# A fused attention and expert kernel on eight cores: who makes -alpha k, and a new order on TensorE, VectorE and ScalarE

## The chip, the cores and the metric

The kernel runs on the 8 cores of one Trainium2 chip. Each core computes two of the sixteen sequences and shares nothing with the others. A core has five engines with queues of their own: TensorE (PE), VectorE (DVE), ScalarE (ACT), GpSimd (POOL) and SyncE (SP), which only issues DMAs here. The metric is the device time in microseconds of the slowest core.

## What is computed

```python
x = x + attention(layernorm(x))
x = x + experts(layernorm(x))

# attention, 16 heads of 64, chunks of 64 tokens
q, k, v = x @ Wq.T, x @ Wk.T, x @ Wv.T;  k = k / max(|k|, 1e-12)
alpha = sigmoid(alpha_raw) * 0.5;  beta = sigmoid(beta_raw) * 2.0
for each chunk:
    attn_out = softmax(causal(q @ k.T / 8)) @ v
    out = attn_out + 0.1 * (q @ M)
    for each token t of the chunk:
        M = M - alpha * outer(M @ k_t, k_t) + beta * outer(v_t, k_t)
out = out @ Wo.T
```

The recurrence over the 64 tokens of a chunk is solved at once: with the strictly lower triangle A of -alpha k k^T, the sum of its powers is applied as (I+A)(I+A^2)(I+A^4)(I+A^8)(I+A^16)(I+A^32).

## The kernel before

The kernel has two phases. Phase A, the attention, takes about 1000 us; phase B, the experts, the rest, and it isn't touched. Phase A runs 32 tiles (NT) of 128 rows, which are one chunk of 64 tokens of both sequences. It is written as a software pipeline in which every engine has its own loop, `for i in range(-1, NT + 3)` (GpSimd's and SyncE's from 0), and an instruction order set out by hand. All order between engines is by counting semaphores. In iteration i an engine works on up to four tiles: it projects tile i (k, v and q, from L495), makes the gram and score products of tile j = i-1, solves tile u = i-2 (powers of A, and their factors) and ends tile e = i-3 (factors 4 and 5, the state, the output product with Wo).

TensorE's order in a full iteration (L714 to L800): k's first half, power_a(1), factor(e,4); k's second half, power_b(1), factor(e,5); v's first half, power_a(2), state_h; half of v's second half, power_b(2), state_m; the rest of v, x_turn (the transpose of the next tile), power_a(3), k_by_h; q's first half, power_b(3), factor(u,0), row_sums; half of q's second half, k_turn, gram_and_scores(j), factor(u,1); the rest of q, wo_part, power_a(4), factor(u,2), q_turn, wo_part, power_b(4), queries, wo_part, power_a(5), factor(u,3), values.

- state_h (from L634, H) makes the update of H from Wf, the result of the last factor, and RHS. VectorE adds it to H_sb (L868). state_m (L647, M) needs the new H_sb's semaphore, since it reuses the PSUM tile psY; VectorE adds it to M_sb (L880). k_by_h (L658) needs both and reads ka_fm, which is -alpha k; VectorE makes RHS of it (L886).
- power_a and power_b (L597) write psX; ScalarE copies them to A[k] and B[k] (L411, L415). VectorE's plus_eye (L825) makes AI[k] = A[k] + I, both inputs in SBUF. factor(u,k) (L630) multiplies with AI[k]; VectorE copies psW to W or, for k = 5, Wf (L829).
- gram_and_scores (L575) writes k k^T and k q^T of every head into the whole of psXY: the heads in row order hrow 0 to 7 into psX, 8 to 15 into psY. Its waits are for -alpha k (s_ka), q_fm, for B[3]'s copy, which frees psX, and for s_lden, the logarithm of the softmax's row sums, which frees psY.
- ScalarE takes the row sums' logarithm and its negative exponential into rden (L475, L477), copies the gram to g_sb (L483), and takes the exponential of the scores into PT (L484), for which power_a(4) waits. ln_steps (L403) are two activations for the layernorm of tile i+2; the norm of k is rk (L459, L461), from VectorE's kss (L871) and its maximum, kmax (L873). o_copy (L435) opens its iteration.
- VectorE's xnf copy (L883) takes x_turn's result and frees psD0 for q's first half. stats and normal (L808 to L811, L817) are the layernorm of tile i+2. k_fm (L898) is the copy of k_turn's result.
- GpSimd multiplies elementwise: PT by the mask (L363), -alpha k (kaq, L367), k squared (L372), k by its norm (kt, L376), Ms_sb = M_sb by beta (L381), Pn = PT by rden (L391), and two masks for A[0] and B[0] (L395, L398). Between them it issues eight DMAs of each tile (cast, L354) that turn the experts' weights into bf16.

## Time and profile before

| | us |
|---|---|
| median of 3 runs | 1400.66 (1400.26 to 1402.19) |
| the profiled execution: time | 1394.15 |
| its span on the slowest core | 1392.3 (cores 1382.8 to 1392.3) |
| TensorE busy over the span | 1148.8 (83%) |
| VectorE, ScalarE, GpSimd busy | 980.6 (70%), 810.8 (58%), 672.1 (48%) |

| stage, us | TensorE busy | VectorE | ScalarE | GpSimd | granted clock |
|---|---|---|---|---|---|
| 360 to 460 | 91.36 | 74.20 | 57.05 | 71.84 | 1.00 |
| 560 to 660 | 89.95 | 71.95 | 56.10 | 71.29 | 1.00 |
| 760 to 860 | 89.44 | 70.97 | 56.42 | 71.51 | 1.00 |
| 1100 to 1392 | 240.21 | 217.07 | 205.98 | 10.30 | 0.93 |

The columns of the second table are the busy time of each engine within the stage. TensorE's granted clock is given as a share of full speed, 2.4 GHz. The attention loop lies between about 64 and 1005 us. An iteration begins with k's first half; the full ones took 27.1 to 31.5 us from one to the next, mostly 27.7 to 29.7. An engine that is not the bottleneck may sit idle at no cost, so the shares of busy time alone don't tell what a change is worth.

### The profile page before, as it was taken

The page shows a single profiled execution, that of the slowest core. Times are in us where ns is not written, and L with a number is a line of the kernel's source. Part 1 is how long each engine was busy: PE and PEld are TensorE (multiplying, and loading weights), DVE is VectorE, ACT ScalarE, POOL GpSimd, SP SyncE. Part 2 cuts the span into 40 slices and gives each one's busy share as a digit, 9 for nine tenths or more (in the row PEclk, how much of TensorE's full clock was granted, in tenths as well). Part 3 has the DMA queues.
Part 4 walks back from the last instruction along what each step waited for, and adds up shares of the span by engine and source line. Part 5 has one row for each costly group of instructions (what it writes and reads, how often), then busy time and mean ns, then how long its engine had stood idle before and what let it go on. Part 6 is the DMA issues. An engine that isn't in the chain of part 4 may idle for free. (4 is left out here: it accounts for less than half of the span.)

```text
span 1392.3 us, 68142 instructions; the slowest of 8 cores (1382.8 to 1392.3 us)
## 1 busy us (share of the span) xinstructions
PE 1148.8 (83%) x28864; PEld 692.5 (50%) x28864; DVE 980.6 (70%) x1389; ACT 810.8 (58%) x1187; POOL 672.1 (48%) x566
## 2 busy tenths in 40 slices
PE   1578988889899988889899888885677779887798
PEld 0245555555555555555555555553344556544665
DVE  3167777677777777777777777765778587785776
ACT  0155656555565555555565555654249776488775
POOL 4166766776767766777667766675101000011000
PEclk9799999999999999999999999996569799988999
DMA  9912222222222222222222222123134485750947
GB/s 160 149 44 45 43 51 51 52 48 49 47 51 55 45 49 53 47 53 43 52 50 53 50 47 40 30 34 79 23 94 143 134 263 164 217 184 35 312 135 235
DMA packets 75158, 122.09 MB, mean 88 GB/s; under 512 B 13408, under 2 KB 38000, under 8 KB 74864
## 3 DMA queue, kind: packets, MB, share of 16 engines
q1 hardware_dynamic: 48128, 92.30, 21.8%
q0 software_dynamic: 26736, 25.44, 13.6%
q8 instruction: 237, 3.88, 1.1%
q14 instruction: 57, 0.47, 0.1%
HBM read 117.93 MB, written 41.94 MB: 115 GB/s over the span
## 5 line engine op out<-in xcount | busy, mean ns | idle before, releaser
L829 DVE CAST W<-psW 128x1024 bf16<-128x1024 f32 x160 | 195.5, 1222 | 112.6 <-PE psW L630 112.4
L415 ACT CAST B<-psXY 128x1024 bf16<-128x1024 f32 x128 | 129.9, 1015 | 74.0 <-PE psXY L597 74.0
L1095 POOL TENSOR_TENSOR psel<-permT_sb,gmask_sb 128x256 bf16<-128x256 bf16 x32 | 20.1, 628 | 260.8 <-DVE permT_sb L1327 235.9
L411 ACT CAST A<-psXY 128x1024 bf16<-128x1024 f32 x128 | 129.8, 1014 | 21.2 <-PE psXY L597 21.0
L517 PE MATMUL psD<-wv_sb,xnf 128*128 128x512 bf16 x512 | 128.8, 386 | 13.6 <-DMA wv_sb<-wvT 13.6
L540 PE MATMUL psD<-wq_sb,xnf 128*128 128x512 bf16 x512 | 128.6, 385 | 11.8 <-DMA wq_sb<-wqT 6.4
L508 PE MATMUL psD<-wk_sb,xnf 128*128 128x512 bf16 x512 | 123.6, 386 | 14.6 <-DMA wk_sb<-wkT 11.8
L825 DVE TENSOR_TENSOR AI<-A,eye 128x1024 bf16<-128x1024 bf16 x160 | 131.1, 834 | 1.8 <-ACT A L411 1.3
L569 PE MATMUL psD<-wo_sb,o_fm 128*128 128x512 bf16 x512 | 131.3, 391 | 0.7 <-issue 0.6
L376 POOL TENSOR_TENSOR kt<-kraw,rk 128x1024 bf16<-128x1024 f32 x32 | 60.8, 1902 | 134.4 <-ACT rk L461 134.4
L1108 ACT CAST R<-P 128x1024 bf16<-128x1024 f32 (+1 forms) x128 | 110.1, 905 | 8.3 <-PE P L1187 6.2
L391 POOL TENSOR_TENSOR Pn<-PT,rden 128x1024 bf16<-128x1024 bf16 x32 | 68.6, 2142 | 91.1 <-ACT rden L477 91.1
L1340 DVE CAST R<-P 128x512 bf16<-128x512 f32 x128 | 81.2, 685 | 28.5 <-PE P L1214 28.2
L597 PEld LDWEIGHTS psXY<-A,B 64*64 64x64 bf16 x5120 | 57.1, 110 | 76.0 <-issue 72.9
L597 PE MATMUL psXY<-A,B 64*64 64x64 bf16 (+1 forms) x5120 | 74.9, 194 | 17.1 <-ACT PT L484 7.9
L630 PE MATMUL psW<-W,AI 64*64 64x64 bf16 x5120 | 75.7, 197 | 14.6 <-DVE W L829 7.7
L435 ACT CAST o_fm<-psXY 128x1024 bf16<-128x1024 f32 x32 | 32.4, 1012 | 94.3 <-PE psXY L684 94.3
L1144 ACT COPY ring<-P 128x1024 bf16<-128x1024 bf16 x64 | 64.6, 1012 | 37.0 <-PE P L1228 37.0
L429 ACT CAST q_tm<-psD 128x512 bf16<-128x512 f32 x64 | 37.6, 587 | 82.1 <-PE psD L540 82.1
L363 POOL TENSOR_TENSOR PT<-PT,mj 128x1024 bf16<-128x1024 bf16 x32 | 68.4, 2136 | 30.7 <-DVE AI L825 30.7
L372 POOL TENSOR_TENSOR sq_sb<-kraw 128x1024 f32<-128x1024 f32 x32 | 60.6, 1893 | 45.9 <-ACT kraw L419 28.4
L1187 PE MATMUL P<-psel,xy 64*128 64x256 bf16 x512 | 58.6, 310 | 28.5 <-ACT R L1108 22.9
(138 smaller groups left out, 2578.7 us busy)
## 6 DMA issues: line engine op xcount, KB each, us to landing
ring<-f1d SPq DMA_DIRECT2D x64, 256.0 KB, 4.0
ring<-f2d SPq DMA_DIRECT2D x64, 256.0 KB, 5.0
out<-ring SPq DMA_DIRECT2D x64, 256.0 KB, 3.4
xy<-x SPq DMA_DIRECT2D x68, 128.0 KB, 2.4
f1d<-f1w POOLq DMA_DIRECT2D x128, 64.0 KB, 2.6
f2d<-f2w POOLq DMA_DIRECT2D x128, 64.0 KB, 2.7
x1d<-x1b SPq DMA_DIRECT2D x64, 128.0 KB, 2.4
xy<-x1d SPq DMA_DIRECT2D x32, 256.0 KB, 3.5
```

Source lines behind the costliest of these rows:

```text
L411: s.copy(A[k][:], psX).then_inc(s_a, 1)
L415: s.copy(B[k][:], psX).then_inc(s_b, 1)
L508: ins = t.matmul((psD0, psD1)[hf][:, :], xn_fm[i % 2][:, kc * 128:(kc + 1) * 128], wk_sb[:, kc * 1024 + hf * 512:kc * 1024 + hf * 512 + 51 ...
L517: ins = t.matmul((psD0, psD1)[hf][:, :], xn_fm[i % 2][:, kc * 128:(kc + 1) * 128], wv_sb[:, kc * 1024 + hf * 512:kc * 1024 + hf * 512 + 51 ...
L540: ins = t.matmul((psD0, psD1)[hf][:, :], xn_fm[i % 2][:, kc * 128:(kc + 1) * 128], wq_sb[:, kc * 1024 + hf * 512:kc * 1024 + hf * 512 + 51 ...
L569: ins = t.matmul((psD0, psD1)[hf][:, :], o_fm[:, oc * 128:(oc + 1) * 128], wo_sb[:, oc * 1024 + hf * 512:oc * 1024 + hf * 512 + 512], star ...
L597: ins = t.matmul(psX[c:c + 64, hr * 64:hr * 64 + width], left[k][r:r + 64, hr * 64:hr * 64 + 64], right[k][r:r + 64, hr * 64:hr * 64 + width],
L630: ins = t.matmul(psW[c:c + 64, hr * 64:hr * 64 + 64], AI[k][r:r + 64, hr * 64:hr * 64 + 64], w_old, start=True, stop=True, tile_position=( ...
L825: v.tensor_tensor(heads(AI[k][:, :]), heads(A[k][:, :]), by_mask(eye2), ALU.add).then_inc(s_ai, 1)
L829: v.tensor_copy((Wf if k == 5 else W[k % 2])[:], psW[:, 0:1024]).then_inc(s_w, 1)
L1108: s.copy(gather_place(n, q)[:, 0:h, :, :], gathered_ps(q)[:, 0:h, :, :]).then_inc(s_ga, 1)
L1340: v.tensor_copy(place(2 * p)[:, 4 * hf:4 * hf + 4, :, :], half_tiles(P[u % 3][:, 0:512])).then_inc(s_iv, 1)
```

## The change

-alpha k is no longer one product on GpSimd at the start of the next iteration: ScalarE makes it at the end of the same iteration, in eight activations of 128 columns with a scale per partition, between power_b(4)'s copy and the next iteration's o_copy. On TensorE state_h goes ahead of power_a(2), and state_m ahead of power_b(2). gram_and_scores takes the heads in row order, and waits for s_lden only ahead of the ninth. On ScalarE ln_steps goes between rden's logarithm and its exponential. On VectorE plus_eye(0) and (1) go ahead of factor(e,5)'s copy, M_sb ahead of plus_eye(2) and kmax behind it, and k_fm ahead of normal.

```diff
--- before.py
+++ after.py
@@ -362,11 +362,6 @@
                     g.wait_ge(s_exp, u + 1)
                     g.tensor_tensor(heads(PT[u % 2][:, :]), heads(PT[u % 2][:, :]), by_mask(mj), ALU.mult).then_inc(s_ptm, 1)
                 cast(u, 0)
-                if 0 <= j < NT:
-                    g.wait_ge(s_kfm, j + 1)
-                    g.tensor_tensor(ka_fm[j % 3].rearrange("p (a t) -> p a t", a=8),
-                                    k_fm[j % 3][:, :].rearrange("p (a t) -> p a t", a=8),
-                                    nega[:, :].unsqueeze(2).broadcast_to([128, 8, 128]), ALU.mult).then_inc(s_ka, 1)
                 if i < NT:
                     g.wait_ge(s_kraw, 2 * i + 2)
                     g.tensor_tensor(sq_sb[:], kraw[:], kraw[:], ALU.mult).then_inc(s_sq, 1)
@@ -428,6 +423,16 @@
                     s.wait_ge(s_tq, i)
                 s.copy(q_tm[:, hf * 512:hf * 512 + 512], (psD0, psD1)[hf][:, :]).then_inc(s_q, 1)
 
+            def minus_alpha(i):
+
+                s.wait_ge(s_kfm, i + 1)
+                if i == 0:
+                    s.wait_ge(s_prep, PREP)
+                for a in range(8):
+                    ins = s.activation(ka_fm[i % 3][:, a * 128:a * 128 + 128], k_fm[i % 3][:, a * 128:a * 128 + 128],
+                                       AF.Copy, scale=nega[:, a:a + 1])
+                ins.then_inc(s_ka, 1)
+
             s.wait_ge(s_prep, 2)
             ln_steps(0)
             def o_copy(e):
@@ -466,13 +471,14 @@
                     q_half(i, 0)
                 if solve:
                     power_b(u, 3)
-                if i + 2 < NT:
-                    ln_steps(i + 2)
                 if solve:
                     s.wait_ge(s_pden, u + 1)
                     if u > 0:
                         s.wait_ge(s_pn, u)
                     s.activation(rden[:], psY, AF.Ln).then_inc(s_lden, 1)
+                if i + 2 < NT:
+                    ln_steps(i + 2)
+                if solve:
                     s.wait_ge(s_lden, u + 1)
                     s.activation(rden[:], rden[:], AF.Exp, scale=-1.0).then_inc(s_rec, 1)
                 if i == -1:
@@ -487,6 +493,8 @@
                 if solve:
                     power_a(u, 4)
                     power_b(u, 4)
+                if proj:
+                    minus_alpha(i)
                 if i >= NT + 1:
                     choice_ln(s, env, 2 * (i - NT - 1))
                     choice_ln(s, env, 2 * (i - NT - 1) + 1)
@@ -578,9 +586,10 @@
                 t.wait_ge(s_qfm, j + 1)
                 if j > 0:
                     t.wait_ge(s_b, 4 * (j - 1) + 3)
-                    t.wait_ge(s_lden, j)
-                for h in range(NH):
+                for h in sorted(range(NH), key=hrow):
                     r, hr = (h % 2) * 64, hrow(h)
+                    if hr == 8 and j > 0:
+                        t.wait_ge(s_lden, j)
                     for s in range(2):
                         c = (h // 2) * 128 + s * 64
                         ins = t.matmul(psXY[s * 64:s * 64 + 64, hr * 128:hr * 128 + 128], k_fm[j % 3][r:r + 64, c:c + 64],
@@ -737,17 +746,17 @@
                     t.wait_ge(s_wv, 16)
                 if proj:
                     v_part(i, 0, 0, 8)
-                if solve:
-                    power_a(u, 2)
                 if ends:
                     state_h(e)
+                if solve:
+                    power_a(u, 2)
 
                 if proj:
                     v_part(i, 1, 0, 4)
-                if solve:
-                    power_b(u, 2)
                 if ends:
                     state_m(e)
+                if solve:
+                    power_b(u, 2)
 
                 if proj:
                     v_part(i, 1, 4, 8)
@@ -859,25 +868,26 @@
                                     eye2[:, 0:32].unsqueeze(1).broadcast_to([128, 16, 32]), ALU.add).then_inc(s_ai, 1)
                     factor(e, 3)
                     factor(e, 4)
-                    factor(e, 5)
                 if solve:
                     plus_eye(u, 0)
                     plus_eye(u, 1)
                 if ends:
+                    factor(e, 5)
                     v.wait_ge(s_ph, e + 1)
                     v.tensor_add(H_sb[:], H_sb[:], psY).then_inc(s_h, 1)
                 if proj:
                     v.wait_ge(s_sq, i + 1)
                     v.reduce_sum(kss[:, :].unsqueeze(2), heads(sq_sb[:, :]), axis=AX).then_inc(s_kss, 1)
-                    v.wait_ge(s_kss, i + 1)
-                    v.tensor_scalar_max(kss[:], kss[:], 1e-24).then_inc(s_kmax, 1)
-                if solve:
-                    plus_eye(u, 2)
                 if ends:
                     v.wait_ge(s_pm, e + 1)
                     if e > 0:
                         v.wait_ge(s_ms, e)
                     v.tensor_add(M_sb[:], M_sb[:], psY).then_inc(s_m, 1)
+                if solve:
+                    plus_eye(u, 2)
+                if proj:
+                    v.wait_ge(s_kss, i + 1)
+                    v.tensor_scalar_max(kss[:], kss[:], 1e-24).then_inc(s_kmax, 1)
                 if i + 1 < NT:
                     v.wait_ge(s_tx, i + 2)
                     v.tensor_copy(xn_fm[(i + 1) % 2][:], psT).then_inc(s_xfm, 1)
@@ -891,11 +901,11 @@
                 if solve:
                     plus_eye(u, 3)
                     factor(u, 0)
+                if proj:
+                    v.wait_ge(s_tk, i + 1)
+                    v.tensor_copy(k_fm[i % 3][:], psT).then_inc(s_kfm, 1)
                 if i + 2 < NT:
                     normal(i + 2)
-                if proj:
-                    v.wait_ge(s_tk, i + 1)
-                    v.tensor_copy(k_fm[i % 3][:], psT).then_inc(s_kfm, 1)
                 if solve:
                     factor(u, 1)
                 if i == -1:
```

## Rows read from the trace of the kernel before

**Rows 1.** Waits between 60 and 950 us: total us, times, longest.
```profile
PE psXY L668 <- DVE M_sb L880: 22.9, 28, 1.4
...
PE psXY L586 <- ACT rden L475: 18.5, 29, 0.7
```

**Rows 2.** Timeline of TensorE: start us, us, engine, line, operation, count, [idle before].
```profile
773.76 0.45 PE L597 MATMUL psXY<-A,B 64*64 64x64 bf16 x32
774.18 0.45 PE L642 MATMUL psXY<-RHS,Wf 64*64 64x64 bf16 x32
...
780.20 1.89 PE L540 MATMUL psD<-wq_sb,xnf 128*128 128x512 bf16 x8
...
785.77 0.45 PE L630 MATMUL psW<-W,AI 64*64 64x64 bf16 x32
...
788.30 0.45 PE L597 MATMUL psXY<-A,B 64*64 64x64 bf16 x32 [0.24 <-ACT PT L484]
788.70 0.45 PE L630 MATMUL psW<-W,AI 64*64 64x64 bf16 x32
```

**Rows 3.** Timeline of VectorE in the same iteration.
```profile
775.08 1.21 DVE L868 TENSOR_TENSOR H_sb<-H_sb,psXY 128x1024 bf16<-128x1024 bf16 x1
...
777.52 0.17 DVE L873 TENSOR_SCALAR kss<-kss 128x16 f32<-128x16 f32 x1
...
779.37 0.69 DVE L883 COPY xnf<-psD 128x1024 bf16<-128x1024 bf16 x1
780.38 1.22 DVE L886 TENSOR_TENSOR RHS<-vt,psXY 128x1024 bf16<-128x1024 bf16 x1 [0.33 <-PE psXY L668]
...
783.03 0.67 DVE L825 TENSOR_TENSOR AI<-A,eye 128x1024 bf16<-128x1024 bf16 x1
...
784.75 0.81 DVE L817 TENSOR_SCALAR xn_tm<-xy,mv,rstd 128x1024 bf16<-128x1024 f32 x1
```

**Rows 4.** Timeline of GpSimd in the same iteration.
```profile
778.46 1.90 POOL L376 TENSOR_TENSOR kt<-kraw,rk 128x1024 bf16<-128x1024 f32 x1 [3.96 <-ACT rk L461]
...
780.86 1.91 POOL L381 TENSOR_TENSOR Ms_sb<-M_sb,b 128x1024 bf16<-128x1024 bf16 x1
...
786.54 2.14 POOL L391 TENSOR_TENSOR Pn<-PT,rden 128x1024 bf16<-128x1024 bf16 x1 [2.79 <-ACT rden L477]
...
789.18 2.14 POOL L395 TENSOR_TENSOR A<-g_sb,mlo 128x1024 bf16<-128x1024 bf16 x1
```

**Rows 5.** Timeline of ScalarE in the same iteration.
```profile
784.16 1.02 ACT L475 ACTIVATE rden<-psXY 128x1024 f32<-128x1024 f32 x1
785.28 1.06 ACT L477 ACTIVATE rden<-rden 128x1024 f32<-128x1024 f32 x1
```

**Rows 6.** Timeline of GpSimd and VectorE in iteration 30.
```profile
898.43 1.92 POOL L381 TENSOR_TENSOR Ms_sb<-M_sb,b 128x1024 bf16<-128x1024 bf16 x1
...
898.88 2.03 DVE L825 TENSOR_TENSOR AI<-A,eye 128x1024 bf16<-128x1024 bf16 x1
```

**Rows 7.** Groups of ScalarE over the span: count | busy us, mean ns | idle before, releaser.
```profile
L435 ACT CAST o_fm<-psXY 128x1024 bf16<-128x1024 f32 x32 | 32.4, 1012 | 94.3 <-PE psXY L684 94.3
...
L1114 ACT ACTIVATE inner<-P,bias_sb 128x128 bf16<-128x128 f32 x64 | 23.6, 368 | 20.3 <-PE P L1199 17.5 <-PE P L1214 2.3
```

**Rows 8.** The instructions of L137: ns min/median/max, first and last start.
```profile
L137 DVE TENSOR_SCALAR xy<-xy,mv_y,rstd_y x32: 525/534/920, 1006.8 to 1259.1; 128x1024 bf16<-128x1024 bf16 x32
```

**Rows 9.** Timeline of VectorE and GpSimd at 1028 us.
```profile
1028.35 0.92 DVE L137 TENSOR_SCALAR xy<-xy,mv_y,rstd_y 128x1024 bf16<-128x1024 bf16 x1
...
1028.38 0.61 POOL L1095 TENSOR_TENSOR psel<-permT_sb,gmask_sb 128x256 bf16<-128x256 bf16 x1 [4.52 <-DVE permT_sb L1327]
```

**Rows 10.** Timeline of VectorE and GpSimd in the start-up, iteration 2.
```profile
103.26 3.19 DVE L825 TENSOR_TENSOR AI<-A,eye 128x1024 bf16<-128x1024 bf16 x1
...
103.77 2.13 POOL L398 TENSOR_TENSOR B<-g_sb,mup 128x1024 bf16<-128x1024 bf16 x1
```

**Rows 11.** Timeline of TensorE in iteration 32, the first without a projection.
```profile
949.32 0.64 PE L642 MATMUL psXY<-RHS,Wf 64*64 64x64 bf16 x32 [0.35 <-DVE Wf L829]
```

More of the change, by code:

```diff
@@ L739, in pe @@
                     v_part(i, 0, 0, 8)
+                if ends:
+                    state_h(e)
                 if solve:
                     power_a(u, 2)
-                if ends:
-                    state_h(e)
                 if proj:
                     v_part(i, 1, 0, 4)
+                if ends:
+                    state_m(e)
                 if solve:
                     power_b(u, 2)
-                if ends:
-                    state_m(e)
                 if proj:
@@ L893, in dve @@
                     factor(u, 0)
-                if i + 2 < NT:
-                    normal(i + 2)
                 if proj:
@@ L898, in dve @@
                     v.tensor_copy(k_fm[i % 3][:], psT).then_inc(s_kfm, 1)
+                if i + 2 < NT:
+                    normal(i + 2)
                 if solve:
```

## The prediction

> **What bounds the kernel now.** I read the table of stages first: the attention loop takes about 900 of 1392 us, on every core alike, so 0.3 us in each of its iterations is worth 9 us. Next the waits of TensorE in that loop [rows 1]: two stand out, k_by_h for VectorE's M_sb and the gram product for ScalarE's rden. Then one iteration on each engine in order of time. I use the one from 767 to 795 us; it has hardly any gap that comes from TensorE's own queue, and the differences below recur within 0.1 us in the others. TensorE [rows 2] works in long runs and stops at M, at k_by_h, at gram and at power_a(4). So it is close to being the bound, but what sets its stops is two chains of other engines. The first is VectorE's [rows 3]: H_sb, kss, kmax, plus_eye(2), M_sb, xnf without a gap, and q_part starts 0.14 us after xnf's end. The second is ScalarE's, from q_part's end to the exponential that power_a(4) waits for. GpSimd [rows 4] is idle half of the time and seems to bound nothing, but it matters below. I write p0 to p4 for plus_eye(u,0..4), Pn, Ms for the GpSimd products of L391 and L381, W0, W1 for VectorE's copies of factor(0), factor(1).
>
> **H and M ahead, VectorE's order.** H now starts where power_a(2) started, 773.76 instead of 774.18 [rows 2]. It takes 0.45, VectorE answers 0.13 later: H_sb at 774.34, where before it waited for p0 and p1 until 775.08. p0 and p1 go into the gap before the copy of factor(5); they overlapped a GpSimd product there and don't in the new place, so they are no longer in the way. An operation of 1.21 us gives way to the next after 1.13, one of 0.69 after 0.61. So kss 775.47, M_sb 776.60, p2 777.73, kmax 778.34, and xnf 0.11 later, 778.45. TensorE would reach k_by_h at about 778.3 and finds M_sb ready at 777.96: that wait goes. Late next is xnf: q_part starts 0.83 after xnf's start (779.37 to 780.20 before [rows 2, 3]), so at 779.28. **Gain up to q_part 0.92 us**, not the sum of the M and k_by_h stops, since xnf was 0.6 us behind them all along.
>
> **Gram in two waits, ScalarE's order.** The half of gram that writes psX can start right after k_turn, and the other half when Ln has read psY. This removes the stop of 0.6 us, 18.5 us over 29 times [rows 1], but the next thing that TensorE needs is power_a(4), which waits for the last exponential. ScalarE has no idle time from q_part's end to there, so only what shortens ScalarE's own chain counts. With ln_steps between Ln and Exp the step from Ln to Exp, 1.12 us [rows 5], no longer has its 0.2 of waiting for its own result. **Gain 0.20** at power_a(4): it could start at 788.30 - 0.92 - 0.20 = 787.18. Pn, which waits for Exp, moves by the same: 786.54 to 785.42 [rows 4].
>
> **minus_alpha.** Eight activations with a pointer scale of 128x128. The nearest row is L1114, 128x128 with a pointer bias, 0.368 each [rows 7], so at most 8 x 0.37 = 2.9 us; from below 8 x 0.2. It stands after B4 and ahead of o_copy, where ScalarE idles 94.3 / 32 = 2.9 us [rows 7]. I take nothing, and if it ran over, kraw's copy has another 1 us of idle before it. On GpSimd 1.9 us go; the next product there waits for kraw anyhow, so no gain. The Trainium skill, page ScalarE: Activation LUTs, section What ACT_TABLE_LOAD costs, gives 280 + 0.833 N ns with a pointer operand and an overlap of 93 ns; as an estimate that is 8 x 0.29 = 2.4 us, inside the same idle time, so the sum stays.
>
> **What the rearrangement brings together.** This decides the sign. A plus_eye reads two SBUF tensors. Alone it takes 0.67, but where it meets a GpSimd product it doesn't end until that one has: in the iteration from 884 us Ms ran from 898.43 to 900.35, p3 started at 898.88 and ended at 900.91, 0.56 after it [rows 6]. Where do Ms and p3 fall in the new order? Before, kmax starts at 777.52, kt at 778.46, Ms at 780.86 [rows 3, 4]: Ms is kmax + 3.34, through ScalarE's two small activations, kt and one DMA issue. p3 was at 783.03, kmax + 5.51. Now p2 (0.61), M_sb (1.13) and RHS's wait (0.41 with its overlap) no longer stand between kmax and p3: kmax + 3.36. So Ms starts at 781.68 and p3 at 781.70. Ms ends at 783.59, and p3 at 784.15 instead of 782.37.
> From p3's end to normal's start there were 784.75 - 783.70 = 1.05 us, with W0 between; now k_fm, 0.60, stands there too. So W0 ends at 785.29 and normal is due at 785.81. factor(1) can't start before W0's end + 0.14 = 785.43; before, power_a(4) came 788.30 - 0.24 - 785.77 = 2.29 after factor(1)'s start [rows 2], so it now comes at 787.72, not 787.18. This collision alone leaves a gain of 0.58.
> But Pn runs from 785.42 to 787.56, and normal is due 0.39 after its start. normal (L817) reads 1024 f32 in 0.81, while kss's reduction of as many takes 1.21, so it is in a faster form. The only row of such a tensor_scalar that meets a GpSimd product at its start is L137: 0.53 alone, 0.92 when the product of 0.61 began 0.03 after it, that is, it ended 0.29 after the product did [rows 8, 9]. So I take normal to be held too. Of its 0.81, 0.53 remain when Pn ends (as 0.56 of p3's 0.67 remained): normal ends at 788.09, W1 starts at 788.00 and ends at 789.23, and factor(2) starts at 789.37, against 788.70 before. From factor(2) on the iteration is TensorE's own work, as before. **Each iteration is 0.67 us longer.**
> Bounds of this step: below, no hold of either (-1.12 us); above, normal loses again to the mask product that follows Pn after 0.50 us [rows 4]. Row for that: p4 at 103.26 in the start-up took 3.19, because a product that began 0.51 after it went first [rows 10].
> Here the Trainium skill has a rule. Page SBUF — State Buffer, section Who interferes with whom: VectorE's two-input SBUF operations and two-port forms share a port pair with GpSimd, and whichever starts first has it for its whole instruction. By that rule normal, waiting at Pn's end, is next, which is the +0.67; the row of 3.19 us speaks against it, and by it the result is the second rival below.
>
> **The last iterations.** In the two without a projection TensorE idles and the chain of powers sets the time. There H waits for Wf [rows 11], idle 0.35 after a power product of 0.64, and power_a(2) is now queued behind it: about 1.5 us each, +3 together (0 to 4). In iterations 30 and 31 there are no stats and no normal, p3 met Ms already [rows 6], and the gain of 1.1 each comes: -2.
>
> **Sum.** Iterations 3 to 29 are full ones: 27 x 0.67 = +18; -2 +3: +19 us. On the profiled execution, 1394.15, that gives 1413; the median of the runs is 6.5 higher, 1400.66, so **1419 us**. The feed-forward half is untouched.
>
> **Rivals.** (a) Neither hold happens, because Ms is 0.6 us later or p3 earlier than I place them: 29 x -1.12 + 3 = -29, 1371 us. For it: the waits that go are real and the lead of Ms is 0.02 us only; against it: p3 was held where it started up to 0.45 after Ms, and it would have to be a whole plus_eye ahead. (b) p3 is held, but normal isn't, as its form may not collide or Pn is later by 0.4: 27 x -0.58 - 2 + 3 = -15, 1386 us. Both end faster, the first by the change's own mechanism. (c) normal is held through the mask product too: that runs from 788.06 to 790.19, normal ends at 790.75, factor(2) starts at 792.03, 3.33 later than before: +90, 1491 us. Through both mask products, 2.63 more: 5.96, 1562 us. It decides from whether 0.50 us between two products is enough for an operation that needs 0.53. (d) minus_alpha is dear: only from 2.9 + 1 us, 0.5 each, would it touch kraw, so it is in no sum.
>
> **How the numbers follow.** Forecast 0.35; (a) 0.16; (b) 0.17; (c) 0.25, of which 0.15 for one mask product; about 0.07 for holds that cancel the gain. A measurement of this kernel tells some 0.2% from no change. Range: from (a), 1367, to (c) with one mask product, 1492; outside is the dearest case, 0.10, and some of the rest. Faster 0.34 ((a), (b) and a little), same 0.04, slower 0.62. The likeliest case's own range, with the tail's bounds and 0.1 us either way per iteration, is 1414 to 1424.
>
> **What the profile will show.** Right: k_by_h no longer waits for M_sb, q_part waits for xnf, gram hardly waits; L825 has a longer mean, some of 2.4 us, beginning with Ms; L817 has 2.3 us instead of 0.81; factor(2) waits for W1. If L825 and L817 keep 0.68 and 0.81, (a) is right; if L817 alone does, (b); if L817 takes 4 us or more, (c). What would make it wrong: an iteration whose kmax, Ms and p3 stand elsewhere than I put them, as each hold hangs on tenths of a microsecond.

## The result, and the profile after

The changed kernel takes 1406.62 us (median of 5 runs, 1403.83 to 1407.42) against 1400.46 of the kernel before on the same chip: a ratio of 1.004, 95% interval 1.0026 to 1.0055. It is slower by 6 us, where 19 were forecast. Its profiled execution took 1407.42 us, with spans of 1396.8 to 1405.9 us. Some lines have moved: plus_eye is L834, normal L826, the copies of the factors L838, Ms L376, Pn L386, factor L639, k_by_h L677, minus_alpha L432.

The waits of TensorE between 60 and 950 us answer to [rows 1] (total us, times, longest):

```profile
PE psW L639 <- DVE W L838: 30.3, 31, 1.7
...
PE psXY L606 <- issue: 16.3, 18, 1.6
...
PE psD L548 <- DVE xnf L893: 9.9, 15, 1.2
```

The wait of k_by_h for M_sb (22.9 us) and that of the gram product for rden (18.5) are gone. In their place factor(1) and factor(2), which share the first of these rows, wait for VectorE's copies in front of them, and q_part waits for xnf. One iteration, which begins at 749.91 us, shows how. VectorE, as in [rows 3]:

```profile
761.37 0.17 DVE L890 TENSOR_SCALAR kss<-kss 128x16 f32<-128x16 f32 x1
761.45 0.68 DVE L893 COPY xnf<-psD 128x1024 bf16<-128x1024 bf16 x1
...
764.72 2.45 DVE L834 TENSOR_TENSOR AI<-A,eye 128x1024 bf16<-128x1024 bf16 x1
767.10 1.21 DVE L838 CAST W<-psW 128x1024 bf16<-128x1024 f32 x1
768.23 0.68 DVE L906 COPY kf<-psD 128x1024 bf16<-128x1024 bf16 x1
768.83 2.22 DVE L826 TENSOR_SCALAR xn_tm<-xy,mv,rstd 128x1024 bf16<-128x1024 f32 x1
770.97 1.21 DVE L838 CAST W<-psW 128x1024 bf16<-128x1024 f32 x1
```

GpSimd beside it, as in [rows 4]:

```profile
764.70 1.92 POOL L376 TENSOR_TENSOR Ms_sb<-M_sb,b 128x1024 bf16<-128x1024 bf16 x1
...
768.36 2.14 POOL L386 TENSOR_TENSOR Pn<-PT,rden 128x1024 bf16<-128x1024 bf16 x1 [0.78 <-ACT rden L483]
770.44 0.71 POOL L354 DMA_DIRECT2D f2d<-f2w  x1
```

p3 starts with Ms and lasts 2.45 us instead of 0.67, to 0.55 after Ms's end. normal starts 0.47 into Pn and lasts 2.22 instead of 0.81; the DMA issue behind Pn is stretched from 0.54 to 0.71, so normal goes first there. TensorE and ScalarE, as in [rows 2] and [rows 5, 7]:

```profile
749.88 1.42 PEld L516 LDWEIGHTS psD<-wk_sb,xnf 128*128 128x128 bf16 x8 [0.17 <-issue]
750.13 1.67 PE L516 MATMUL psD<-wk_sb,xnf 128*128 128x512 bf16 x7 [0.31 <-issue]
...
762.25 1.42 PEld L548 LDWEIGHTS psD<-wq_sb,xnf 128*128 128x128 bf16 x8 [0.41 <-issue]
762.49 1.67 PE L548 MATMUL psD<-wq_sb,xnf 128*128 128x512 bf16 x7 [0.55 <-DVE xnf L893]
...
768.57 0.64 PE L639 MATMUL psW<-W,AI 64*64 64x64 bf16 x32 [1.04 <-DVE W L838]
...
772.44 0.45 PE L639 MATMUL psW<-W,AI 64*64 64x64 bf16 x32 [1.03 <-DVE W L838]
```
```profile
775.71 2.44 ACT L432 ACTIVATE kaq<-kf,nega 128x128 bf16<-128x128 bf16 x8
778.35 1.01 ACT L440 CAST o_fm<-psXY 128x1024 bf16<-128x1024 f32 x1 [0.20 <-PE psXY L693]
```

This core's trace lacks the record of the first matmul of k's and of q's group (x7 beside eight weight loads, PEld). By the loads, which the rows of before show 0.03 us ahead of their matmuls, the iteration begins at 749.91 and q_part at 762.27. In us from the iteration's start, the prediction's places against these rows:

| | forecast | after | before |
|---|---|---|---|
| q_part | 12.40 | 12.36 | 13.32 |
| p3, start and end | 14.82, 17.27 | 14.81, 17.26 | |
| normal, start and end | 18.93, 21.21 | 18.92, 21.14 | |
| factor(2) | 22.49 | 22.53 | 21.82 |

So the order of events is the predicted one, and this iteration reaches factor(2) 0.71 us later than the clean one of before, where 0.67 was forecast. But the mean iteration doesn't lose that much. I took the first start of k, q_part, power_a(4) and factor(2) in the iterations between 120 and 900 us, 26 on each of the 8 cores, 208 in all, from the records of TensorE (means, us):

| | period | k to q_part | to power_a(4) | to factor(2) | to the next k |
|---|---|---|---|---|---|
| before | 28.74 | 13.74 | 8.06 | 0.42 | 6.51 |
| after | 29.01 | 13.12 | 8.28 | 1.12 | 6.48 |
| after, the 110 with normal held | 28.95 | 12.79 | 8.39 | 1.77 | 6.00 |
| after, the 98 with normal free | 29.07 | 13.49 | 8.16 | 0.39 | 7.02 |

The last two rows are the puzzle. An iteration whose normal is held (2.2 to 2.8 us) is 0.9 us later at factor(2) than one whose normal is free (0.8 us), and yet takes no longer from k to k. Something evens the two out.

**Where it goes.** It is in the rows of the waits that end with "issue", that is, in which TensorE waited for nothing that the profile shows. On the cores whose records of matmuls are complete, all of them over 0.3 us in the loop stand at one place of TensorE's instruction stream: where a page of 256 instructions ends. (Where the first matmul of a group isn't recorded, the rows show gaps of up to 0.4 us that are none.) The profile has a DMA queue for these pages:

```profile
q0 software_dynamic: 2152, 1.77, 14.6%
...
q8 instruction: 22, 0.36, 1.6%
```

That is 22 fetches of 16 KB in 100 us (600 to 700, after). I counted TensorE's queue from its records, a matmul as two instructions (its weight load and itself) and a wait as one: an iteration has 1585, or 6.2 pages. A fetch's DMA takes 1.05 us (median), but the page's first instruction hardly ever runs earlier than 2.2 us after the start of the fetch (in about 1% of the pages, and never under 2.1); where there is a stop it is 2.5 us (median), where there is none, 3.1. So a stop appears when TensorE comes to the end of a page within some 2.3 us of the next one's fetch. Where TensorE waits for another engine shortly before, the fetch can be done in the meantime. TensorE's idle time shows the exchange (120 to 900 us, mean of the cores, us an iteration):

| | waits for other engines | stops at page ends | period |
|---|---|---|---|
| before | 2.23 | 0.79 | 28.74 |
| after | 1.80 | 1.33 | 29.01 |
| after, normal held | 2.75 | 0.49 | 28.95 |
| after, normal free | 0.72 | 2.29 | 29.07 |
| e4 | 1.05 | 1.71 | 28.75 |

The held and the free iterations weren't assigned by an edit: the free ones have 1.18 us of stops ahead of q_part already and the held ones 0.42, so a stop may be what frees normal. What the two rows show is that the sum of both kinds hardly moves.

The iterations with at most 0.15 us of stops show the change without them. There are 46 of the 208 before and 37 after, and their means are 27.97 and 28.66: 0.69 us longer, where 0.67 was forecast.

The next table gives the stops between 400 and 880 us, the mean of the 8 cores (over 0.3 us at a page's end, in the stream of weight loads; and 480 us divided by the pages run). The matmuls, which run behind the loads, stood idle there for less: 0.11 us a page before, 0.23 after, 0.29 in e4, 0.44 in e10.

| | ratio to before | share of pages with a stop | stops, us a page | us a page in all |
|---|---|---|---|---|
| before | 1 | 0.23 | 0.18 | 4.66 |
| after | 1.004 | 0.33 | 0.30 | 4.70 |
| e1 | 1.019 | 0.26 | 0.23 | 4.81 |
| e2 | 1.001 | 0.42 | 0.38 | 4.67 |
| e3 | 1.001 | 0.40 | 0.35 | 4.69 |
| e4 | 1.004 | 0.39 | 0.38 | 4.68 |
| e7 | 1.000 | 0.25 | 0.23 | 4.68 |
| e9 | 1.016 | 0.34 | 0.32 | 4.76 |
| e10 | 1.045 | 0.50 | 0.55 | 4.64 |
| e11 | 1.012 | 0.19 | 0.13 | 4.71 |
| e12 | 1.019 | 0.36 | 0.32 | 4.84 |

The Trainium skill, page Runtime: NRT & Kernel Launch, section Instruction fetch mechanics, states that each sequencer fetches blocks of 256 instructions by a DMA queue of its own, and that crossing a block costs one tail-bump, mostly hidden. The blocks and the queue agree with this trace; "mostly hidden" holds for 77% of the pages before and no longer for 42% of them in e2.

### The profile page after: what moved, and what is told of

It is laid out like the page before. It is cut to its first block and busy times, and to the rows that moved or that the text cites. A ratio compares the mean times of both kernels' runs of the same rounds, so it can differ in the third digit from the quotient of the medians.

```text
span 1405.9 us, 68061 instructions; the slowest of 8 cores (1396.8 to 1405.9 us)
## 1 busy us (share of the span) xinstructions
PE 1110.2 (79%) x28558; PEld 700.5 (50%) x28864; DVE 1012.6 (72%) x1389; ACT 883.0 (63%) x1443; POOL 617.0 (44%) x534
## 5 line engine op out<-in xcount | busy, mean ns | idle before, releaser
L838 DVE CAST W<-psW 128x1024 bf16<-128x1024 f32 x160 | 195.0, 1218 | 87.8 <-PE psW L639 87.8
L834 DVE TENSOR_TENSOR AI<-A,eye 128x1024 bf16<-128x1024 bf16 x160 | 143.6, 913 | 2.3 <-ACT A L406 1.8
L548 PE MATMUL psD<-wq_sb,xnf 128*128 128x512 bf16 x450 | 114.9, 385 | 24.8 <-DVE xnf L893 9.9
L516 PE MATMUL psD<-wk_sb,xnf 128*128 128x512 bf16 x453 | 112.1, 390 | 26.0 <-DMA wk_sb<-wkT 12.4
L525 PE MATMUL psD<-wv_sb,xnf 128*128 128x512 bf16 x423 | 109.1, 386 | 28.3 <-issue 14.6
L577 PE MATMUL psD<-wo_sb,o_fm 128*128 128x512 bf16 x448 | 117.0, 392 | 7.9 <-issue 6.4
L639 PE MATMUL psW<-W,AI 64*64 64x64 bf16 x5120 | 77.6, 197 | 46.3 <-DVE W L838 38.2
L386 POOL TENSOR_TENSOR Pn<-PT,rden 128x1024 bf16<-128x1024 bf16 x32 | 71.4, 2232 | 49.4 <-ACT rden L483 49.4
L639 PEld LDWEIGHTS psW<-W,AI 64*64 64x64 bf16 x5120 | 62.6, 110 | 56.2 <-issue 54.1
L414 ACT COPY kraw<-psD 128x512 f32<-128x512 f32 x64 | 37.4, 585 | 69.6 <-PE psD L516 69.5
```

Source lines behind the costliest of these rows:

```text
L516: ins = t.matmul((psD0, psD1)[hf][:, :], xn_fm[i % 2][:, kc * 128:(kc + 1) * 128], wk_sb[:, kc * 1024 + hf * 512:kc * 1024 + hf * 512 + 51 ...
L525: ins = t.matmul((psD0, psD1)[hf][:, :], xn_fm[i % 2][:, kc * 128:(kc + 1) * 128], wv_sb[:, kc * 1024 + hf * 512:kc * 1024 + hf * 512 + 51 ...
L548: ins = t.matmul((psD0, psD1)[hf][:, :], xn_fm[i % 2][:, kc * 128:(kc + 1) * 128], wq_sb[:, kc * 1024 + hf * 512:kc * 1024 + hf * 512 + 51 ...
L577: ins = t.matmul((psD0, psD1)[hf][:, :], o_fm[:, oc * 128:(oc + 1) * 128], wo_sb[:, oc * 1024 + hf * 512:oc * 1024 + hf * 512 + 512], star ...
L639: ins = t.matmul(psW[c:c + 64, hr * 64:hr * 64 + 64], AI[k][r:r + 64, hr * 64:hr * 64 + 64], w_old, start=True, stop=True, tile_position=( ...
L834: v.tensor_tensor(heads(AI[k][:, :]), heads(A[k][:, :]), by_mask(eye2), ALU.add).then_inc(s_ai, 1)
```

## The experiments

Times are ratios to the kernel before on the same chip, with 95% intervals.

**e1: the two DMA issues behind Ms put ahead of it**, in the changed kernel, so that Ms starts 1 us later.

```diff
                 cast(u, 2)
+                cast(u, 3)
+                cast(u, 4)
                 if 0 <= e < NT - 1:
...
-                cast(u, 3)
-                cast(u, 4)
```

> The changed kernel with one edit on GpSimd: both DMA issues that followed the Ms product are made ahead of it, so Ms starts 1.04 us later and plus_eye(3) has 1 us free of GpSimd products; nothing moves on the other engines. Theory (the holds of plus_eye(3) and of the layernorm's normal by GpSimd cost what H and M ahead had won): plus_eye(3) takes 0.7 us, normal mostly 0.8, factor(2) follows power_a(4) after 0.4 us, an iteration takes 28.74 - 0.62 - 0.2 = 27.9 us on average, ratio to the kernel before 0.982 to 0.990 (1376 to 1386 us). Rival (the holds are there, but TensorE is late for another reason, such as its own queue or ScalarE's longer work): the ratio stays at 1.002 to 1.006 though the holds are gone. Second rival (a later Ms holds normal instead): plus_eye(3) is short, normal has 1.5 us or more, ratio 0.99 to 1.0.

1.0188 (1.0162 to 1.0214). p3 isn't free at all, but held longer, and normal in 193 of 200 iterations. VectorE and GpSimd in one of them:

```profile
716.12 3.23 DVE L834 TENSOR_TENSOR AI<-A,eye 128x1024 bf16<-128x1024 bf16 x1
```
```profile
715.34 1.04 POOL L354 DMA_DIRECT2D f1d<-f1w  x2
716.37 0.50 POOL L354 DMA_DIRECT2D f2d<-f2w  x1
716.88 1.91 POOL L378 TENSOR_TENSOR Ms_sb<-M_sb,b 128x1024 bf16<-128x1024 bf16 x1
```

p3 began 0.76 us before Ms and needs 0.67, and still ended 0.56 after Ms. So a product behind a DMA issue holds VectorE from the issue on (more below). From q_part to power_a(4) it took 9.46 us instead of 8.28, and the iteration 29.75. So the period is 0.74 us longer than in the changed kernel, and the stops at the ends of pages became fewer again (0.30 to 0.23 us a page, 0.4 us an iteration). The granted clock in the loop fell too, from 0.999 to 0.985 (120 to 900 us, mean of the cores). At 26 us of TensorE's work an iteration that is at most 0.4 us of the 0.74, so what the holds alone cost isn't separated from it.

**e2: plus_eye(3) ahead of the statistics**, meant to have it done, or nearly, before Ms starts; **e3: normal behind the copy of factor(1)**, so that factor(2) doesn't wait for it; **e4: both**.

```diff
+                if solve:
+                    plus_eye(u, 3)
                 if i + 2 < NT:
                     stats(i + 2)
                 if solve:
-                    plus_eye(u, 3)
                     factor(u, 0)
...
-                if i + 2 < NT:
-                    normal(i + 2)
                 if solve:
                     factor(u, 1)
+                if i + 2 < NT:
+                    normal(i + 2)
```

> The changed kernel with one edit on VectorE: plus_eye(3) goes ahead of the layernorm's two statistics, so it should run and end before Ms begins. Theory of the holds: plus_eye(3) 0.7 us, the copy of factor(0) as early as in the first experiment, normal about 0.8 us as it now comes 0.9 us ahead of Pn, ratio 0.980 to 0.990. Rival (TensorE late for another reason): 1.002 to 1.006. If plus_eye(3) is short but normal still meets Pn in some iterations, the ratio is between, 0.988 to 0.996.

> The changed kernel with only normal moved, behind the copy of factor(1); plus_eye(3) still meets Ms. This splits the two holds. Theory: normal is held as before or longer (Pn or the first mask product), but factor(2) no longer waits for it: power_a(4) to factor(2) falls from 1.12 to 0.4 us, an iteration from 29.01 to 28.3 to 28.4 us, ratio to the kernel before 0.988 to 0.993. What remains of the gain lost is plus_eye(3)'s part, 0.3 to 0.5 us an iteration. Rival (the second hold counts for nothing since the copy of factor(1) was late anyway): 1.001 to 1.006.

> Both edits on VectorE together: plus_eye(3) ahead of the statistics, normal behind the copy of factor(1). Theory: the full gain of H and M ahead and of the gram's two waits, 0.62 and 0.2 us an iteration, 27 iterations and some 2 us more: ratio 0.980 to 0.988 (1372 to 1384 us). If the first hold alone was the cause, it equals the run with plus_eye(3) moved alone within 0.1%. Rival: no better than 0.995, if an earlier q_part only makes TensorE wait longer for ScalarE's last exponential.

e2 1.0012 (0.9988 to 1.0037), e3 1.0013 (0.999 to 1.0036), e4 1.0037 (1.0016 to 1.0059). The second edit does what it was made for, the first in part. In e2 normal is held in 6 iterations of 208 (half of its group on the slowest core, with a mean of 805 ns, is below), but p3 still in 137 of 214, for 1.16 us in the mean against 1.81 in the changed kernel and 0.67 alone. In e3 and e4 factor(2) follows power_a(4) after 0.36 and 0.41 us:

```profile
L826 DVE TENSOR_SCALAR xn_tm<-xy,mv,rstd 128x1024 bf16<-128x1024 f32 x15 | 12.1, 805 | 0.1
```

Their fastest iterations show a gain: the tenth percentile is 27.27 in e2 and 27.25 in e4, against 27.86 before, about half of the 1.12 us of the prediction's first rival. The five iterations of e4 with at most 0.15 us of stops took 26.97, 1.00 less than such iterations of before. But the mean stays at 28.81, 28.83 and 28.75 against 28.74. In e4 TensorE waits 1.2 us an iteration less for other engines than before, and 0.9 of it stands in the stops instead. The waits of TensorE in e4 between 120 and 900 us:

```profile
PE psXY L606 <- issue: 16.7, 20, 1.6
PE psW L639 <- issue: 7.9, 16, 1.1
PE psXY L709 <- issue: 7.2, 8, 1.5
```

and one of them in its timeline, in the midst of the 32 matmuls of one product, which wait for nothing:

```profile
715.22 0.28 PE L606 MATMUL psXY<-B,A 64*64 64x64 bf16 x11
716.59 0.35 PE L606 MATMUL psXY<-B,A 64*64 64x64 bf16 x21 [1.08 <-issue]
```

In e3 and e4 normal starts later and meets Pn's end. In 11 of their iterations it began with the DMA issue behind Pn, and each time it was held through both mask products, for 5.8 to 5.9 us. One of them (e3, core 3), VectorE and GpSimd:

```profile
757.78 5.86 DVE L826 TENSOR_SCALAR xn_tm<-xy,mv,rstd 128x1024 bf16<-128x1024 f32 x1
```
```profile
757.78 0.54 POOL L354 DMA_DIRECT2D f2d<-f2w  x1
...
760.96 2.13 POOL L393 TENSOR_TENSOR B<-g_sb,mup 128x1024 bf16<-128x1024 bf16 x1
```

**e5, e6: nearly no weight traffic in the loop.** Do the fetches lose to the bytes of the weight conversion, which share the DMA engines? e5 is e4, e6 the kernel before, each with all conversions ahead of GpSimd's loop, and DMAs of 8 columns in their places, so that the issues stay.

```diff
-            def cast(u, part):
+            def cast(u, part, width=8):
...
-                g.dma_start(out=w_d[r:r + 64, c:c + 512], in_=w_h[r:r + 64, c:c + 512]).then_inc(s_cast, 16)
+                g.dma_start(out=w_d[r:r + 64, c:c + width], in_=w_h[r:r + 64, c:c + width]).then_inc(s_cast, 16)
+
+            for n in range(NT):
+                for part in range(8):
+                    cast(n, part, 512)
+            g.wait_ge(s_cast, 16 * 8 * NT)
...
```

> The kernel with plus_eye(3) ahead of the statistics and normal behind the copy of factor(1), and with the bytes of the weights' conversion moved: all 256 DMAs are made and waited for before GpSimd's loop, and in the loop each is issued again over 8 columns instead of 512, so GpSimd's queue keeps its timing and the loop has hardly any software DMA traffic. The total is about 300 us longer for the wait in front; what counts is an iteration's length and the gaps at the ends of TensorE's instruction pages in the loop. In the first four experiments these gaps had grown from 1.15 to about 2.1 us an iteration as TensorE's waits for semaphores went. Theory A (the fetch of an instruction page is late because it shares the DMA engines with the conversion): gaps fall below 1.0 us, an iteration takes 27.4 to 27.8 us. Theory B (the fetch has a time of its own and TensorE runs through dense pages faster than that): gaps stay at 1.8 to 2.2 us, an iteration at 28.5 to 28.8.

> The kernel before with the same move of the conversion's bytes to the front, as the partner of the run above. Theory A: its gaps of 1.15 us an iteration fall below 0.6, an iteration takes 28.1 to 28.3 instead of 28.74. Theory B: both stay. In either case the difference between the two kernels with the conversion in front tells what H and M ahead, the gram's two waits and the two moves are worth without the traffic: 0.6 to 0.9 us an iteration by A, below 0.2 by B.

The whole is longer, 1.1224 and 1.118, since the conversions now come first; what counts is the loop. The DMA queues of e5, 600 to 700 us:

```profile
q0 software_dynamic: 2160, 0.03, 2.7%
...
q8 instruction: 21, 0.34, 1.4%
```

The conversions' share of the DMA engines is down from 14.6% to 2.7%, and a fetch still takes 1.05 us. The pages took 4.59 us in e5 and 4.60 in e6 (400 to 950 us), with 0.30 and 0.14 us of stops each. So most of the stops aren't made by that traffic. Some may be: in the same stretch e4 has 1.83 us of them an iteration (in the matmuls) and e5 1.59, before 0.78 and e6 0.60, and both iterations became shorter, to 28.51 and 28.52 us. For the kernel before that lies between my two theories. e4's order brings nothing over that of before without the traffic either.

**e7: gram in two waits and ScalarE's new order alone**, in the kernel before.

```diff
-                    t.wait_ge(s_lden, j)
-                for h in range(NH):
+                for h in sorted(range(NH), key=hrow):
                     r, hr = (h % 2) * 64, hrow(h)
+                    if hr == 8 and j > 0:
+                        t.wait_ge(s_lden, j)
...
```

> The kernel before with two parts of the change alone: the gram in row order with its second wait ahead of the ninth head, and ln_steps between rden's logarithm and exponential. The prediction's step: TensorE's stop before gram (0.6 us) goes, but ScalarE's chain brings power_a(4) only 0.2 us forward; ratio 0.995 to 0.998. Rival 1 (the whole stop is won): 0.985 to 0.990. Rival 2 (what a stop gives back comes again as gaps at the ends of instruction pages): 0.998 to 1.002, with the gaps up by 0.1 to 0.6 us an iteration.

0.9998 (0.998 to 1.0016). The gram product's wait, 17.6 us in the same stretch of before, doesn't appear any more; the stops rise from 0.18 to 0.23 us a page.

**e8: e4 with the powers ahead of H and M again where there is no projection.**

```diff
-                if ends:
+                if ends and proj:
                     state_h(e)
                 if solve:
                     power_a(u, 2)
+                if ends and not proj:
+                    state_h(e)
...
```

> The kernel with both moves (plus_eye(3) ahead of the statistics, normal behind the copy of factor(1)) and with the power products ahead of H and M, as in the kernel before, in the iterations that project nothing; a full iteration is unchanged. It measures the prediction's term for the last iterations, +3 us (0 to 4). Theory: 2 to 4 us less than the same kernel without this edit (ratio 1.0037), so 0.999 to 1.002; rival (the queue there doesn't matter): 1.003 to 1.005.

1.0019 (0.999 to 1.0047), against e4's 1.0037: 2.5 us less, in the direction and about the size of the +3 us that I gave to the last iterations, but the intervals overlap. It stays open.

**e9, e10, e11: the same time in few instructions or in many.** If pages count, the number of instructions must matter, and not their duration alone. In 29 iterations e9 adds four matmuls of 128x512 (8 instructions) to e4, e11 the same to the kernel before, and e10 adds 64 small matmuls (128 instructions) to e4.

```diff
+                for r in range(4 if hf == 1 and e + 3 < NT else 0):
+                    t.matmul(psD1[:, :], o_fm[:, 0:128], wo_sb[:, 512:1024], start=True, stop=True)
```
```diff
+                again = 2 if k == 3 and 0 < u < NT - 2 else 0
-                for h in range(NH):
+                for h in list(range(NH)) * (1 + again):
```

> The version with both moves (plus_eye(3) ahead of the statistics, normal behind the copy of factor(1)), and in 29 iterations four more matmuls of 128x512 ahead of the second half's output projection. Their result is overwritten by the group that follows, so nothing of the output changes. They are 4 x 0.216 = 0.86 us of TensorE, but only 8 instructions of its queue. Theory 'supply': TensorE's page-end stops (2.1 us an iteration in this version, at some 40% of the pages of 256 instructions) shrink where work is put ahead of them; the addition costs 0.4 to 0.65 us an iteration, the time is 1.011 to 1.017 of the kernel before and the stops fall to 1.6 to 1.9 us an iteration. Theory 'plain': the stops are a fixed cost of every page end, the addition costs its full 0.86 us in each of 29 iterations, 25 us: 1.0037 + 0.018 = 1.0215 of the kernel before, stops unchanged at 2.1.

> The same version, and in 29 iterations the 32 small matmuls (64x64) of factor(3) issued three times over instead of once, with the same result. That is 64 x 12.5 ns = 0.80 us more of TensorE, about as much as the four long matmuls of the sister run, but 128 instructions of its queue, half a page more in each iteration (6.2 pages before). Theory 'supply': what counts is pages, at some 4.4 us each at the least: up to 0.5 x 4.4 = 2.2 us an iteration where the stretch is bound by supply, 1.2 to 2.2 us an iteration in the mean, 35 to 64 us: 1.028 to 1.050 of the kernel before. Theory 'plain': 0.80 us x 29 = 23 us, as with the long matmuls: 1.020.

> The kernel before with the same four long matmuls. Its page-end stops are 1.15 us an iteration, at some 25% of the pages. Theory 'supply': there is less to absorb the addition: 0.5 to 0.75 us of the 0.86 an iteration show, 1.010 to 1.016; the step from the kernel before is larger than the step from the version with both moves. Theory 'plain': the full 25 us, 1.018, the same step as in the other.

e9 1.016 (1.0119 to 1.02), e10 1.0448 (1.04 to 1.0495), e11 1.0124 (1.0069 to 1.018). **e10 decides.** Its addition is at most 0.80 us of work an iteration (a group of 96 took 1.06 us, one of 32 takes 0.45). The mean iteration goes from 28.75 to 31.04, +2.29, and the time from 1.0037 to 1.0448, 58 us or 2.0 in each of the 29: at least two and a half times the work. Even the fastest tenth of the iterations took 1.9 us more (27.25 to 29.17). It isn't VectorE's or ScalarE's wait; the rows that grew are TensorE's own (120 to 900 us, slowest core):

```profile
PE psW L640 <- issue: 23.2, 32, 2.0
PE psXY L606 <- issue: 18.5, 23, 1.6
PE psXY L694 <- issue: 12.1, 6, 3.1
```

Half of the pages have a stop, and 0.55 us a page are lost, but a page takes 4.64 us, as before (4.66). The stretch from 560 to 660 us of before (core 5) and of e10 (core 0) shows it: busy time and instructions of TensorE, its weight loads, VectorE, ScalarE, GpSimd, then the granted clock:

```profile
560.00:660.00 100.00, 89.95 (x2649) 52.26 (x2639) 71.95 (x88) 56.10 (x76) 71.29 (x57) 1.00 0.25 50
```
```profile
560.00:660.00 100.00, 86.10 (x2710) 51.05 (x2694) 68.34 (x84) 60.33 (x102) 61.33 (x51) 0.98 0.24 47
```

TensorE runs about as many matmuls in 100 us (2649 and 2710), though an iteration now has 64 more: the iteration grew with its instructions. The clock of 0.98 adds to it; at 26 us of TensorE's work an iteration, 2% are at most 0.5 us of the 2.29, so the plain account is still short by 1 us. In TensorE's idle time the stops grew from 1.71 us an iteration to 3.03, while its waits for other engines stayed (1.05 and 0.98).

The long matmuls tell less. The step from e4 to e9 is 1.2%, or 0.6 us for 0.86 of work, and that from before to e11 as large, while the plain account gives 1.8%. By the profiles the mean iteration grew by 0.81 in e9 and by 0.59 in e11, the stops having fallen by 0.06 and 0.05 us a page, some 0.3 us an iteration. The intervals are too wide to say how much of the work was absorbed, and that the kernel before absorbs less than e4, which I expected, isn't seen.

**e12: the H and M part alone**, in the kernel before, with VectorE's first half in the new order; -alpha k stays on GpSimd.

```diff
+                if ends:
+                    state_h(e)
                 if solve:
                     power_a(u, 2)
-                if ends:
-                    state_h(e)
...
                     factor(e, 4)
-                    factor(e, 5)
                 if solve:
                     plus_eye(u, 0)
                     plus_eye(u, 1)
                 if ends:
+                    factor(e, 5)
...
```

> The kernel before with the state part alone: the H and M products ahead of the powers on TensorE, and VectorE's first half in the changed order (M_sb ahead of plus_eye(2), kmax behind it, the copy of factor(5) behind plus_eye(1)). -alpha k stays on GpSimd, gram and normal are as before. The waits of k_by_h for M_sb and of the M products for H_sb (21.5 + 10.2 us in 27 iterations) lie on TensorE's path; the change takes most of the first. My blind account (a clean iteration without stops) gives 0.6 to 0.8 us an iteration, 16 to 22 us, or 0.984 to 0.989. Theory 'supply': the stops take it back: 0.996 to 1.004, with the page-end stops up from 1.15 to about 1.7 us an iteration. A third: kmax later delays kt, k_turn and Ms, and the collision with plus_eye(3) is here too: 1.003 to 1.008.

1.0191 (1.0142 to 1.0241), worse than every one of the three accounts. TensorE's largest wait is a new one (120 to 900 us):

```profile
PE psXY L642 <- DVE Wf L829: 27.9, 15, 3.8
```

VectorE, GpSimd and TensorE in one iteration with it:

```profile
406.31 3.90 DVE L825 TENSOR_TENSOR AI<-A,eye 128x1024 bf16<-128x1024 bf16 x2
410.13 1.21 DVE L829 CAST Wf<-psW 128x1024 bf16<-128x1024 f32 x1
```
```profile
404.89 0.54 POOL L354 DMA_DIRECT2D f1d<-f1w  x1
405.44 1.91 POOL L367 TENSOR_TENSOR kaq<-kf,nega 128x1024 bf16<-128x1024 bf16 x1
407.70 1.97 POOL L372 TENSOR_TENSOR sq_sb<-kraw 128x1024 f32<-128x1024 f32 x1 [0.35 <-ACT kraw L419]
```
```profile
411.71 0.45 PE L642 MATMUL psXY<-RHS,Wf 64*64 64x64 bf16 x32 [2.31 <-DVE Wf L829]
```

p0 and p1, which now stand ahead of the copy of factor(5), meet GpSimd's product for -alpha k and the next one; they take 3.90 us, against 1.89 mostly before and 1.28 in the changed kernel, and H is 2.31 late. Such an iteration is one in three: in 64 of 200 H waited over 1 us for Wf, and these took 31.7 us. The other 136 took 28.6, hardly less than before (28.74), with 1.35 us of stops instead of 0.79. The granted clock in the loop was 0.986 against 0.999, again at most 0.4 us an iteration.

## Why the prediction was right and wrong

**The direction, and the places of all steps, were right.** q_part's gain of 0.92 showed as 0.96 in the clean iteration. p3 met Ms, normal met Pn, factor(2) waited for the copy of factor(1). minus_alpha cost nothing: 2.44 us in the idle time ahead of o_copy, where 2.9 was the bound. (The estimate from the Trainium skill, page ScalarE: Activation LUTs, section What ACT_TABLE_LOAD costs, was 2.4; the trace agrees.) In the changed kernel normal was never held through a mask product, so rival (c) didn't happen here; the 11 rows of e3 and e4 show that what it describes exists, through both products, when normal begins with the DMA issue behind Pn. normal, which began within Pn, took 2.22 us and ended 0.55 after it, ahead of what followed on GpSimd.

**The size of one term was wrong: 0.67 us an iteration, which measured 0.27.** 27 x 0.27 = 7 us, and with -2 and +3 for the last iterations the sum would have been 8; the runs show 6. Two things went into this:

- I took both holds at full length in every iteration. normal was held in 110 of 208, where it began between 0.48 us after Pn's recorded start and 0.07 before it; in the others it began at least 0.09 before Pn and ran its 0.8 us. That nearly halves the term at factor(2): the step from power_a(4) to factor(2) grew by 0.70, where 1.25 was forecast. p3 was held in 205 of 211, but for 1.81 us in the mean and not 2.45.
- I read one iteration because it had hardly any gap of TensorE's own, and multiplied what it gave by 27. **That is the step that failed: the term 27 x 0.67 = +18.** It holds for the iterations without stops (0.69 measured), but those are a fifth of the loop. In the others the stops grow where waits go, from 0.79 to 1.33 us in the mean, and the waits fall by 0.43. q_part came 0.62 us earlier in the mean, not 0.92, and the held and the free iterations took nearly the same time (28.95 and 29.07).

The failed step reaches further than this forecast. The rivals (a) and (b) would have been wrong by much more: e4 comes nearest to the case of (a), for which I gave 1371 us, with normal off TensorE's path and p3's hold shortened. It took 1405. Had the holds not been there, I would have forecast a gain of 2%, and e4 suggests that little of it would have come. The range, 1367 to 1492, came from rivals of the holds alone; that it contains 1407 says nothing for the sum.

**Part by part.** Gram in two waits is worth nothing measurable (e7). H and M ahead, with -alpha k where it was, costs 1.9% (e12), and the whole change costs 0.4%. So to move -alpha k off GpSimd, which I costed at nothing ("no gain"), seems to be worth about 1.5% in this company: p0 and p1 would else be held there. This is a difference of two runs and not an experiment of its own, and a part of it is the lower clock of e12. I had noted that they no longer overlap a GpSimd product in the new place, but not that this is so only because one product is gone. (e12 also lacks the swap of k_fm and normal, which wasn't run alone.)

**What is shown and what is argued.** Shown: the holds; the stops at the ends of pages of 256 instructions; that they grow when waits go (e2 to e4, e7); that most of them don't come from the conversions' traffic (e5, e6); that instructions cost more than their work when there are more of them (e10). Argued: that the supply of pages sets a floor. By the fastest tenth of e2 and e4 it would be near 27.25 / 6.19 = 4.4 us a page; the means stay at 4.64 to 4.70 in before, after, e2, e3, e4, e7 and e10, however they are ordered (4.71 to 4.84 in the others with the traffic in the loop). What starts a fetch isn't visible: it came 0.4 to 2.9 us after the start of the page in front (5th to 90th percentile).

No version here was faster than the kernel before.

## What to carry to other kernels

Look at where the bound engine waits for nothing that the profile shows before you add up its waits: if those gaps come at a fixed count of its instructions, a removed wait may be worth less than its length, here next to none of it, and fewer instructions may bring what a better order can't (no run here tried it). Check a forecast of a loop with the mean of many iterations and not with its cleanest one. And when a VectorE operation with two SBUF inputs is moved, look at what GpSimd has queued at the new place, its DMA issues included.

## What the runs showed of the hardware that I had not expected

**A GpSimd product that is ready holds VectorE from the DMA issue ahead of it.** I looked at every plus_eye that stands alone in the timeline and began while GpSimd issued a DMA (100 to 900 us, 8 cores; before, after, e1 and e12). Where the product behind the issue had no wait, all 258 were held and ended 0.56 us after that product's end, also those that began up to 1.05 us before it and would have been through. Where the product had to wait for a semaphore, none of 398 was held (0.67 to 0.69 us). This is also what the start-up row of 3.19 us shows [rows 10]: a DMA issue ran from 103.21, the product behind it was ready, and the plus_eye that began at 103.26 waited for both. In the prediction that row was the ground for rival (c). It isn't a case of an operation that waits at a product's end, which is what rival (c) needs: normal, waiting at Pn's end, went first each time. But the 11 iterations of e3 and e4 in which normal began with the issue are like it, and there the hold went on through the next issue and the second product. Why normal, by then waiting at a product's end too, didn't go first there, no run tells. By the rule of the Trainium skill, page SBUF — State Buffer, section Who interferes with whom, the one that issues first has the pair for its whole instruction. normal's rows agree with it, to 0.08 us: it was held or not as it began less or more than that ahead of Pn. In the 258 cases VectorE was first by the recorded starts, and it lost: here the measurement decides, or GpSimd's product had claimed the pair before its recorded start, which no run tells apart.

**TensorE's instruction stream is a resource of its own.** Six pages of 256 instructions an iteration, each ready some 2.2 us after its fetch began at the earliest, leave stops of up to 2.0 us, and of up to 3.4 in e10. In the matmuls' idle time they took 0.8 us an iteration before, 3% of the loop, and 3.0 in e10, 10%.
